# BitNet layer of a fused two-layer kernel: 8-bit activations transposed as bfloat16 products with a unit matrix instead of float32 transposes

## Reference

```
def act_quant(x):                       # per token, qb = 128
    scale = qb / clip(max(abs(x)), EPS)
    return clip(round(x * scale), -qb, qb - 1) / scale

gate  = act_quant(x) @ weight_quant(w_gate).T      # weights are -1, 0, 1 times a mean
up    = act_quant(x) @ weight_quant(w_up).T        # 256 -> 1024
inner = silu(gate) * up
y     = act_quant(fwht(inner)) @ weight_quant(w_down).T   # fwht: Hadamard transform of 1024; 1024 -> 256
```

## Time and profile before

| | us |
|---|---|
| median of 3 runs | 569.83 (569.76 to 571.34) |
| profiled execution, its own time | 570.37 |
| profiled execution, span from first to last instruction | 568.6 |
| PE busy in the span | 538.2 |
| DVE, ACT, POOL busy in the span | 389.0, 351.7, 319.9 |

### The profile page before, as it was taken

How to read it: one execution, slowest core, us unless ns; L and a number is a source line. 1 busy time by engine, 2 the same in 40 slices (tenths; PEclk the granted TensorE clock), 3 DMA queues, 4 the chain that set the end, 5 groups by cost and what they waited for, 6 DMA issues and landing times.

```text
span 568.6 us, 9604 instructions
## 1 busy us (share of the span) xinstructions
PE 538.2 (95%) x3232; PEld 463.1 (81%) x3232; DVE 389.0 (68%) x818; ACT 351.7 (62%) x723; POOL 319.9 (56%) x318
## 2 busy tenths in 40 slices
PE   3999998998999999999999999999999979999997
PEld 3777766776878989999999999989998868777886
DVE  4867987589956576656655576646665766877882
ACT  3651144566488686766757565745757655777882
POOL 3579037899448797655544424426698464762320
PEclk9999998999999999999999999989999989999999
DMA  9901135610047768677696767534355734546761
GB/s 284 350 22 54 41 109 169 203 39 1 20 164 229 238 189 256 209 254 223 215 288 192 241 210 225 189 105 156 120 191 152 240 121 139 135 143 186 218 181 39
DMA packets 66673, 95.78 MB, mean 168 GB/s; under 512 B 6337, under 2 KB 38849, under 8 KB 66625
## 3 DMA queue, kind: packets, MB, share of 16 engines
q1 hardware_dynamic: 66624, 95.17, 53.6%
HBM read 67.23 MB, written 27.92 MB: 167 GB/s over the span
## 4 chain that ended last, share of the span: by engine, by line
PE 78%; DVE 7%; POOL 5%; ACT 4%; issue 2%; DMA 2%; SPq 0%; DVEq 0%; POOLq 0%; ACTq 0%
PE ps L1540 22%; PE ps L1541 21%; PE ps L1542 21%; PE ps L1645 4%; PE ps L1750 2%; PE ps L1734 2%; DMA xr<-in_x 1%; PE ps L1757 1%; ACT q2T L915 1%; PE ps L1763 1%; POOL kv_w_lo L574 1%; ACT kv_w_hi L820 1%; DMA k_hl<-k_scratch 1%; DVE xr L1194 1%; DVE a_sel L1180 1%
## 5 line engine op out<-in xcount | busy, mean ns | idle before, releaser
L651 POOL TENSOR_TENSOR probs<-probs,rsum 128x512 f32<-128x512 f32 x64 | 66.6, 1043 | 60.4 <-DVE rsum L1246 60.3
L1241 DVE TENSOR_REDUCE nmax<-ps 128x2 f32<-128x512 f32 x64 | 44.0, 688 | 35.6 <-PE ps L1542 35.3
L953 ACT ACTIVATE probs<-ps,nmax 128x256 f32<-128x256 f32 x128 | 59.8, 481 | 1.6 <-DVE nmax L1241 1.4
L1039 ACT ACTIVATE e_hi<-e_r 128x512 fp32r<-128x512 f32 x64 | 40.3, 630 | 31.5 <-DVE e_r L1466 30.4
L574 POOL TENSOR_TENSOR kv_w_lo<-blk_raw,kv_w_hi 128x1024 fp32r<-128x1024 f32 x16 | 38.9, 2434 | 36.2 <-ACT kv_w_hi L820 36.2
L1466 DVE SCALAR_TENSOR_TENSOR e_r<-ps,cw_row 128x512 f32<-128x512 f32 x64 | 43.5, 684 | 14.6 <-PE ps L1542 13.7
L1232 DVE TENSOR_TENSOR pT_lo<-ps,pT_hi 128x512 fp32r<-128x512 f32 x64 | 43.8, 685 | 11.8 <-ACT pT_hi L959 11.2
L1237 DVE TENSOR_TENSOR oT_lo<-ps,oT_hi 128x512 fp32r<-128x512 f32 x32 | 22.1, 692 | 40.1 <-ACT oT_hi L963 40.1
L774 POOL TENSOR_TENSOR e_lo<-e_sq,e_hi 128x512 fp32r<-128x512 f32 x19 | 24.6, 1294 | 43.2 <-ACT e_sq L1045 38.3
L959 ACT ACTIVATE pT_hi<-ps 128x512 fp32r<-128x512 f32 x64 | 38.3, 601 | 15.5 <-PE ps L1645 15.3
L963 ACT ACTIVATE oT_hi<-ps 128x512 fp32r<-128x512 f32 x32 | 19.1, 597 | 40.7 <-PE ps L1542 40.7
(11 more groups left out here) (292 smaller groups left out, 1873.1 us busy)
## 6 DMA issues: line engine op xcount, KB each, us to landing
cw_row<-cw_scratch SPq DMA_DIRECT2D x64, 256.0 KB, 3.7
v_hl<-v_scratch SPq DMA_DIRECT2D x24, 512.0 KB, 3.6
blk_raw<-in_w_blocks SPq DMA_DIRECT2D x23, 512.0 KB, 4.4
k_scratch<-kv_out SPq DMA_DIRECT2D x32, 256.0 KB, 2.7
v_scratch<-kv_out SPq DMA_DIRECT2D x32, 256.0 KB, 3.2
k_hl<-k_scratch SPq DMA_DIRECT2D x14, 512.0 KB, 3.5
v_scratch<-kv_hi SPq DMA_DIRECT2D x24, 256.0 KB, 2.7
blk_raw<-in_w_tail SPq DMA_DIRECT2D x10, 512.0 KB, 4.6
```

Source lines behind the costliest of these rows:

```text
L651: nc.gpsimd.tensor_tensor(probs[:, b, :, :], probs[:, b, :, :], rsum[:, b, :].unsqueeze(2).to_broadcast([P, 2, S]), ALU.mult).then_inc(pro ...
L953: last = nc.scalar.activation(probs[:, b, t, :], ps[:, S_BANK[b], t * S:(t + 1) * S], ACT.Exp, bias=nmax[:, b, t:t + 1], accum_out=esum[:, ...
L1039: nc.scalar.activation(e_hi[i % 4][:, :], e_r[i % 2][:, :], ACT.Square).then_inc(e_hi_done, 1)
L1241: V.tensor_reduce(nmax[:, b, :], ps[:, S_BANK[b], :].rearrange("p (t k) -> p t k", t=2), AX.X, ALU.max, negate=True).then_inc(max_done, 1)
```

## The change

Both clips write bfloat16 tiles of their own (`q1`, `q2_b`) and take the ROUND off on the way: `(x - ROUND) min 127`. The lower clip is dropped (the scale makes -128 the least value). The transposes of `q1` and `q2_b` become ordinary bfloat16 products in which the data is the stationary operand and a bfloat16 unit matrix `eye_b` is the moving one. ACT makes `eye_b` from `eye` once, after `had`. ACT's copies out of PSUM lose their bias. Waits that follow: ACT's `q2` of a tile waits for the clip of the tile before (PE used to be the reader), DVE's clip waits for the transposes of the tile before, the wait in `quantise(1)` moves behind the multiplications, and PE's Q waits for `eye_b`.

```diff
+        q1 = sb("q1", [P, GN, D], BF16, region)
+        eye_b = sb("eye_b", [P, P], BF16, region)
...
+        q2_b = sb("q2_b", [P, INTER], BF16, part)
...
+            act.wait_ge(ld_const, 16)
             act.wait_ge(ld_had, 16)
...
+            nc.scalar.activation(eye_b[:, :], eye[:, :], ACT.Copy).then_inc(eye_copied, 1)
...
-                nc.scalar.activation(qT[:, g, :, :], ps[:, b:b + 2, :], ACT.Copy, bias=-ROUND).then_inc(q1T_done, 1)
+                nc.scalar.activation(qT[:, g, :, :], ps[:, b:b + 2, :], ACT.Copy).then_inc(q1T_done, 1)
...
-                    nc.scalar.activation(q2T[:, :, :], ps[:, b:b + 2, :], ACT.Copy, bias=-ROUND).then_inc(q2T_done, 1)
+                    nc.scalar.activation(q2T[:, :, :], ps[:, b:b + 2, :], ACT.Copy).then_inc(q2T_done, 1)
...
                     act.wait_ge(s2_ready, i - 1)
+                    if i > 2:
+                        act.wait_ge(q2_clipped, i - 2)
...
-                if g:
-                    dve.wait_ge(q1T_filled, g)
                 for n in range(GN):
                     last = V.tensor_scalar(qtok[:, n, :], h[:, g * GN + n, :], am_r[:, g * GN + n:g * GN + n + 1], ROUND,
                                            ALU.mult, ALU.add)
                 own(last)
-                V.tensor_scalar(qtok[:, :, :], qtok[:, :, :], ROUND + 127.0, ROUND - 128.0, ALU.min, ALU.max).then_inc(q1_ready, 1)
+                if g:
+                    dve.wait_ge(q1T_filled, g)
+                V.tensor_scalar(q1[:, :, :], qtok[:, :, :], ROUND, 127.0, ALU.subtract, ALU.min).then_inc(q1_ready, 1)
...
                     dve.wait_ge(q2_done, i - 1)
-                    V.tensor_scalar(q2[:, :], q2[:, :], ROUND + 127.0, ROUND - 128.0, ALU.min, ALU.max).then_inc(q2_clipped, 1)
+                    if i > 2:
+                        dve.wait_ge(q2T_filled, i - 2)
+                    V.tensor_scalar(q2_b[:, :], q2[:, :], ROUND, 127.0, ALU.subtract, ALU.min).then_inc(q2_clipped, 1)
...
                     pe.wait_ge(q1_ready, n + 1)
+                    pe.wait_ge(eye_copied, 1)
                     for c in range(DC):
                         for j in range(GN):
-                            last = nc.tensor.transpose(ps[:, b + c, j * P:(j + 1) * P], qtok[:, j, c * P:(c + 1) * P], ident)
+                            last = mm(ps[:, b + c, j * P:(j + 1) * P], q1[:, j, c * P:(c + 1) * P], eye_b[:, :], start=True, stop=True)
...
                     for c in range(IC):
-                        last = nc.tensor.transpose(ps[:, b + c // 4, (c % 4) * P:(c % 4 + 1) * P], q2[:, c * P:(c + 1) * P], ident)
+                        last = mm(ps[:, b + c // 4, (c % 4) * P:(c % 4 + 1) * P], q2_b[:, c * P:(c + 1) * P], eye_b[:, :],
+                                  start=True, stop=True)
```

## The result

The changed kernel took 569.03 us as the median of 22 runs (566.07 to 571.26), the kernel before 570.31 on the same chip in the same rounds. The ratio is 0.9972, 95% interval 0.996 to 0.9984: 1.6 us faster by the ratio, 1.3 by the medians, and by a hair less than the 0.3% that I had called the bound of "no change". In two later rounds the same kernel came out at 0.997 (0.9954 to 0.9985) and 0.9982 (0.9963 to 1.0001). Forecast were 3.2 us. So the sign was right, the size half of what I had worked out, and 569.03 lies above my range, which ended at 568.9.

A forecast was written before the change was run, and what follows sets the result against it. PE was taken to set the steps, DVE and POOL close behind, and DVE the stretch 140 to 150. Gains 0.42 + 0.42 + 2.04 + 0.33 = 3.2 us took 569.8 to 566.6; range 564.8 to 568.9.

The forecast's parts named there:

- The rate: PE's ten series of eight transposes: bfloat16 products start 0.056 us apart in place of 0.109, saving 0.42 us a series.
- Rivals 1 and 2: PE's new products start 0.082 us apart (567.9, chance 0.13), or stay at 0.109 with no gain (569.8, chance 0.09).
- Q(0): First Q series on PE, waited for by DVE's additions behind it: saves 0.42 us.
- Q(1) and C(0) to C(3): PE's second Q series and first four C series: each shortens PE's path by 0.42 us.
- the term on POOL: POOL in the steps: 6.38 us busy in 6.41, a lag of a tenth is held, cost 0.
- C(4): C series in step 7: gives only 0.36 us, DVE's remaining idle time ahead of `fT_lo`.
- C(0) to C(4): 2.04: Five C series on PE: up to 2.10 us, limited to 2.04 by DVE's idle time in step 7.
- I take no change: DVE's clips, now bfloat16 out: lengths unchanged, bounds 0.68 to 1.22 us; even at 1.22 a DVE step stays under 6.41.
- the stretch behind as long as before: Sign to look for in the profile after: the stretch behind the steps, set by DVE, keeps its length.
- rival 3: DVE starved by POOL: clips of steps 3 to 7 held to 2.45 us, time 571.8, chance 0.07.
- C(6) and C(7): Last two C series: 0.84 us on PE, but only 0.33 counts, as the first query needs `hT_lo` from DVE.
- rival 4: PE's half-speed clock from 90.0 to 93.4, costing 1.7 us, goes away: 564.9 us, chance 0.06.

The follow-up runs named there:

- after_third: The changed kernel itself, run unchanged in a later round: 569.51 us, ratio 0.9982 to the kernel before.
- fill2: Changed kernel with one filling unit of the shared expert moved from behind H(7) to behind D(5): 568.92 us, ratio 0.9957.
- fill2_before: Kernel before with one filling unit of the shared expert moved from behind H(7) to behind D(5): 569.76 us, ratio 0.9995.
- pair without POOL: Changed kernel and kernel before, each with two POOL instructions let go only behind the last clip: 566.34 us (0.9931) and 569.09 us (0.9971).
- after: The changed kernel in its first measurement against the kernel before: 569.03 us, ratio 0.9972.
- after_again: The changed kernel itself, repeated in a later round: 568.61 us, ratio 0.997 to the kernel before.
- clip_first: Changed kernel with DVE's clip of tile 5 placed ahead of the residual addition in step 7: 569.01 us, ratio 0.9954.
- c_only: Changed kernel with the Q half taken back, only the C series as bfloat16 products: 569.97 us, ratio 0.9989.
- pool_later: Changed kernel with two POOL instructions (low parts of first values and second keys) moved behind the steps: 566.88 us, ratio 0.9938.
- pool_gated: Changed kernel with two POOL instructions moved behind the steps and let go only after the last clip: 566.34 us, ratio 0.9931.

## Why the prediction was half right

Step by step, all at P0 and without falls of the clock:

- *The rate*, 0.056 a product and 0.42 a series: right (0.057). Rivals 1 and 2 are out. The Trainium skill's 81 ns a pair, page "TensorE: Matmul & The Clock Gate", section "Back-to-back issue gap", is not seen here (57). The advice of the Trainium skill, page "Perfetto Trace Analysis", section "Transposes", to use a transpose and not an ordinary matmul, would have kept the float32 transposes, 0.42 us a series slower; a transpose in bfloat16 was not run, so how much of the 0.42 is the type and how much the kind of instruction stays open.
- *Q(0)*: 0.42, measured 0.42. *Q(1) and C(0) to C(3)*, which lie ahead of R5: 5 x 0.42 = 2.10; measured 53.63 - 51.53 = 2.10 (74.46 and 54.83 less 1.2 against 51.51: 2.12). That agreement is in part luck. PE's own way lost 0.2 in the step of 6.60, where the term on POOL ("a lag of a tenth is held. 0") did not hold: `fT_lo` of step 6 starts 134.19 - 83.80 - 1.2 = 49.19 behind the zero before and 131.04 - 83.76 = 47.28 after, 1.91 and not 2.10. The clip behind it then happened to take 1.34 in place of 1.53, and R5 had the 0.19 back.
- *C(4)*: 0.36, DVE's idle time ahead of `fT_lo` in step 7. Of it 0.22 went: from R5 to this `fT_lo` it takes 137.45 - 135.28 = 2.17, before 141.02 - 138.63 = 2.39. The signs had named an idle time of 0.3 to 0.4 in steps 3 to 6; it is 0.39 in steps 3 and 6, and next to none in steps 4 and 5. But **the term "C(0) to C(4): 2.04" was carried through a stretch that DVE sets as if its instructions kept their lengths; the step that failed is the one on the clips, "I take no change", together with "the stretch behind as long as before".** R5 to R6 lost 0.22 of idle time and gained 1.00 in the clip of tile 5: 7.26 became 8.01. Against the forecast of 0.36 less, 1.1 is missing, 1.0 for the clip and 0.1 of idle time that stayed. I had allowed for longer clips at 1.22 a clip and in rival 3 from a clip of 2.0 on, but had priced both by the steps that PE sets. There, clips of 1.44 and 1.67 (steps 3 and 4) left DVE enough room, as argued. In the one stretch where DVE sets the end a single clip is enough.
- *C(6) and C(7)*: 0.33 forecast, nothing measured (R6 to P0 13.57 in both). I had taken the room from `hT_lo` alone. P0 also needs its bank, which ACT's `kv_out` copy frees. In after_third:

```profile
152.69 1.12 ACT L932 ACTIVATE q<-ps,am 128x1024 f32<-128x1024 f32 x1 [1.91 <-DVE am L1375]
153.70 0.59 ACT L832 ACTIVATE kv_out<-ps 128x512 f32<-128x512 f32 x1
154.43 0.47 PE L1549 MATMUL ps<-cT_hi,kv_w_lo 128*128 128x512 f32 x1
...
155.66 0.40 PE L1551 MATMUL ps<-cT_hi,kv_w_hi 128*128 128x512 f32 x1
155.90 0.62 PE L1767 MATMUL ps<-eye_b,q_b 128*128 128x128 bf16 x8
156.10 0.60 ACT L832 ACTIVATE kv_out<-ps 128x512 f32<-128x512 f32 x1 [0.41 <-PE ps L1551]
...
156.84 0.47 PE L1549 MATMUL ps<-hT_hi,wq_lo 128*128 128x512 f32 x1 [0.32 <-ACT kv_out L832]
```

  The same in the kernel before:

```profile
156.32 0.59 ACT L829 ACTIVATE kv_out<-ps 128x512 f32<-128x512 f32 x1
157.06 0.47 PE L1540 MATMUL ps<-cT_hi,kv_w_lo 128*128 128x512 f32 x1
```

  C(6)'s saving is lost first. It brings the filling products behind it 0.3 forward against H(7), up to 153.92; the next one starts at 154.43, 0.51 later where the distance is else 0.23, right behind the end of a `kv_out` copy (154.29). This copy stands in ACT's order behind the `q` of tile 7, and that waits for DVE's scale: a way without C(6). Before, the copy ended at 156.91 and the product began at 157.06. From that product on PE's order is fixed up to the last filling product ahead of C(7); the copy of that one ends at 156.70 and P0 begins 0.14 later, in the kernel before at 159.32 and 159.46, 0.14 later as well. So C(7)'s shorter series only turned into 0.32 us of idle time. That fill2 and fill2_before, with one filling unit less in this place, are the only ones with a shorter way from R6 to P0 (13.24 and 13.25), agrees.
- The sum: 3.21 - 1.1 - 0.33 = 1.8; measured at P0 74.46 - 73.09 + 0.42 = 1.79. For the pair without POOL, where R5 to R6 takes 6.18 and 6.17: 3.21 - 0.33 - 0.35 = 2.53; measured 2.52. The 0.35 is missing there because `fT_lo` comes only 0.17 earlier behind R5 (2.12 for 2.29), and the clip of tile 5 takes 0.90 for 0.74.
- *The copy of the unit matrix*: 0.30, hidden, as forecast. *The clips' output in bfloat16*: free; 0.68 to 0.69 where nothing lies beside it, as in float32. *New waits*: none shows.
- *The clock* (rival 4): the fall at 90 is a matter of the execution, not of the kernel: it is in the profiles of five of these kernels, with and without the change, and missing from the others. It costs 1.2, not the 1.7 I had. Falls at 147 to 150 are a different matter. They are in three of the five profiles in which PE idles for 1.9 us ahead of H(7) (after, after_again, clip_first; not after_third and c_only) and in none of the twelve others. A run's mean clock is lower by 0.003 for each 3.4 us at half speed in 568; counted in that way the kernel before has 2.7 falls a run (112 runs) and the changed kernel 3.1 (46 runs), 0.37 more with a standard error of 0.15. A straight line through the times of these runs gives 0.96 and 1.04 us a fall. So some 0.4 of the 1.8 us probably goes there, and 1.4 is what the first measurement had (1.3 to 1.6); the intervals of the ratios would hold 1.8 us (0.9968) too. The counts of six runs vary more than this difference: pool_later has 1.8, pool_gated 2.8 and still the lowest time.
- *The attention part* moved along, as forecast: from P0 to the end 409.1 us before, 409.4 after, with falls of the clock in the same places (375, 461 and the end).
- Rival 3 had the right mechanism (DVE held by POOL) in the wrong place and at the wrong price: not five steps, one stretch. The Trainium skill, page "SBUF — State Buffer", section "Who interferes with whom", calls the ports shared by VectorE and GpSimd an exclusive lock; the rows agree with that (the clip ends 0.55 behind POOL's instruction, or POOL's is longer by 0.5).

## What to carry to other kernels

Where a speed-up of one engine moves its neighbours in time, look in the stretch that another engine sets for pairs of DVE and POOL instructions that start within a few tenths of each other: which comes first decides who pays (half a microsecond for POOL, a whole one for DVE here), and a list of such pairs from the trace is part of the forecast. Don't move the instruction that is hit, since the wait passes to the next one (clip_first); move the POOL work that needn't be there (pool_gated). And compare traces by distances from a common event, with falls of the clock taken out: these repeated to less than 0.1 us here, while the medians of equal kernels differed by 0.9.

## What was unexpected of the hardware

A tensor_scalar of DVE can be held by a running POOL instruction however short it is: one on four elements a partition took 1.19 to 1.25 us beside POOL and 0.17 alone, and ended when POOL's did. Not every small instruction is: those on one element a partition took 0.20 to 0.21 in the middle of a POOL instruction. Kernel before:

```profile
138.79 1.27 POOL L626 TENSOR_TENSOR fly<-inner 128x512 f32<-128x512 f32 x1 [0.39 <-DVE inner L1356]
...
139.88 0.21 DVE L1366 TENSOR_SCALAR am<-am,c_up 128x1 f32<-128x1 f32 x1
140.02 1.27 POOL L627 TENSOR_TENSOR fly<-inner 128x512 f32<-128x512 f32 x1
...
140.46 0.20 DVE L1369 TENSOR_SCALAR am<-am,fdown 128x1 f32<-128x1 f32 x1
```

The reciprocal of four elements (0.18) wasn't held either. The tensor_tensor of 1024 columns with an operand in PSUM (`fT_lo`) took 1.21 to 1.23 in every row, with POOL or without. A float32 to bfloat16 clip of 1024 columns takes 0.68 to 0.69 us, as long as float32 to float32.
